# Two token tiles through all 64 experts in place, and first-pass steps inside the front end

## The reference

```python
router_probs = softmax(x @ router_w.T + bias)            # 64 experts
topk_p, topk_i = top_k(router_probs, 6)
topk_p = topk_p / (sum(topk_p) + 1e-09)
# each expert takes its tokens in order, up to C = 768 of them (for 4096 tokens)
expert_out = (silu(expert_in @ w_gate) * (expert_in @ w_up)) @ w_down
sparse = segment_sum(gate * expert_out, token)            # 6 terms per token
h = h + shared_out / 2 + sparse
```

## Time and profile before

| | us |
|---|---|
| median of 3 runs | 575.38 (572.39 to 576.1) |
| span of the profiled execution | 575.5 |
| TensorE busy | 418.5 (73%) |
| VectorE busy | 443.7 (77%) |
| ScalarE busy | 281.9 (49%) |
| GpSimd busy | 405.7 (70%) |

### The profile page before, as it was taken

How to read it: one execution, slowest core, us unless ns; L and a number is a source line. 1 busy time by engine, 2 the same in 40 slices (tenths; PEclk the granted TensorE clock), 3 DMA queues, 4 the chain that set the end, 5 groups by cost and what they waited for, 6 DMA issues and landing times.

```text
span 575.5 us, 11745 instructions
## 1 busy us (share of the span) xinstructions
PE 418.5 (73%) x2715; PEld 351.0 (61%) x2715; DVE 443.7 (77%) x1686; ACT 281.9 (49%) x806; POOL 405.7 (70%) x426
## 2 busy tenths in 40 slices
PE   4487867656673429889999999999999999950000
PEld 3356645545562327789899998889888887630000
DVE  5468999999999664978888668988999887485222
ACT  2026355334443306557777787778767574410000
POOL 7770047777777777777777777777777777777773
PEclk9999878869886556889999999999999798995555
DMA  2899801111114214768888898998899876252221
GB/s 82 202 254 233 165 25 50 52 50 52 51 48 133 82 50 124 210 207 246 250 247 234 237 261 245 242 253 242 246 252 250 237 216 162 53 150 73 60 64 41
DMA packets 128296, 91.13 MB, mean 158 GB/s; under 512 B 15224, under 2 KB 118245, under 8 KB 127974
## 3 DMA queue, kind: packets, MB, share of 16 engines
q1 hardware_dynamic: 64230, 38.63, 26.0%
q0 software_dynamic: 13312, 26.59, 16.0%
q10 hardware_dynamic: 50688, 25.17, 14.6%
HBM read 46.99 MB, written 44.04 MB: 158 GB/s over the span
## 4 chain that ended last, share of the span: by engine, by line
DVE 37%; PE 33%; POOL 15%; issue 9%; DMA 3%; ACT 2%; ACTq 0%; POOLq 0%; DVEq 0%
POOL shared L1107 13%; PE bank L458 11%; PE bank L447 10%; PE bank L438 6%; DVE lanes L1028 3%; DVE gate_junk L925 3%; DVE hid L1022 3%; DVE emb L942 2%; POOL emb L1076 2%; DMA emb<-table_dram,idx 2%; DVE x L778 1%; PE bank L347 1%; DVE struck L817 1%; PE bank L397 1%; DVE shared L717 1%
## 5 line engine op out<-in xcount | busy, mean ns | idle before, releaser
L1092 POOL DMA_INDIRECT x_rows<-x,to_row x192 | 190.3, 991 | 93.4 <-issue 58.0
L1107 POOL DMA_INDIRECT shared<-o_rows,to_got x192 | 182.8, 952 | 58.6 <-issue 57.7
L458 PE MATMUL bank<-w_down,hid 64*128 x768 | 112.5, 287 | 8.9 <-DVE hid L1022 8.6
L626 ACT ACTIVATE w_now<-w_in 128x128 f32 x384 | 87.4, 298 | 55.6 <-issue 26.6
L458 PEld LDWEIGHTS bank<-w_down,hid 64*128 64x128 f32 x768 | 94.1, 190 | 22.1 <-issue 13.2
L447 PE MATMUL bank<-x_t,w_now 128*128 128x128 f32 x768 | 106.8, 284 | 0.1
L447 PEld LDWEIGHTS bank<-x_t,w_now 128*128 128x128 f32 x768 | 98.3, 200 | 0.6 <-ACT x_t L629 0.5
L942 DVE SCALAR_TENSOR_TENSOR emb<-shared,gate_of,emb 128x128 f32<-128x128 f32 x192 | 67.2, 351 | 37.7 <-DMA shared<-o_rows,to_got 32.6
L1022 DVE TENSOR_TENSOR hid<-hid,bank 64x512 f32<-64x512 f32 x96 | 66.2, 690 | 35.4 <-ACT hid L634 32.9
L1028 DVE COPY lanes<-bank 128x512 f32<-128x512 f32 x96 | 66.4, 691 | 3.7 <-PE bank L458 0.7
L634 ACT ACTIVATE hid<-bank 64x512 f32<-64x512 f32 x96 | 56.6, 589 | 25.6 <-PE bank L447 21.4
(11 more groups left out here) (210 smaller groups left out, 595.2 us busy)
## 6 DMA issues: line engine op xcount, KB each, us to landing
lanes<-x_rows SPq DMA_DIRECT2D x384, 64.0 KB
o_rows<-lanes ACTq DMA_DIRECT2D x96, 256.0 KB
x_rows<-hid_s SPq DMA_DIRECT2D x2, 2048.0 KB, 17.7
x_rows<-x,to_row POOLq DMA_INDIRECT x192, 2.2
shared<-o_rows,to_got POOLq DMA_INDIRECT x192
w_in<-gate_t_dram SPq DMA_DIRECT2D x1, 2048.0 KB, 23.5
w_in<-up_t_dram SPq DMA_DIRECT2D x1, 2048.0 KB, 31.1
w_down<-down_t_dram SPq DMA_DIRECT2D x2, 1024.0 KB, 15.6
```

Source lines behind the costliest of these rows:

```text
L458: last = pe.matmul(bank_d[k][:, c * P:c * P + P], hid[k][:, c * P:c * P + P], w[:, bass.ds(at[c], P)], start=(c == 0), stop=(c == GROUP - ...
L626: last = act.activation(w_now[k][:, c, :], w[:, bass.ds(at[c], P)], ACT.Copy)
L1092: pool.indirect_dma_start(x_rows, bass.IndirectOffsetOnAxis(ap=to_row[b][:, t * 8 + j:t * 8 + j + 1], axis=0), x3[b][:, t, :], None, bound ...
L1107: pool.indirect_dma_start(got[n % G_RING][:, j, :], None, o_rows[p], bass.IndirectOffsetOnAxis(ap=to_got[b][:, t * 8 + j:t * 8 + j + 1], a ...
```

## The change

Two things are changed together.

1. **Two dense tiles.** The last two token tiles (tiles 2 and 3 of the last sequence) are neither sent nor fetched. They go through all 64 experts where they lie: 32 dense steps of four experts follow the sparse steps, reading `x3_t` (the transposed tokens, left over from the router of the last sequence) and the weights in place. VectorE adds each expert's output times the token's gate (zero where the expert isn't chosen) to the token's row. The last pass has 768 tokens, so 100 tiles and 25 steps: 93 sparse steps, 125 in all.
2. **The front end.** New tables of ticks, with the first sequence's own row; sequence 1 begins 603 ticks and the others 1500 apart. The first five steps (`STEP_AT`) stand inside the front end: on VectorE step 0 comes after `cols` of sequence 5, step 1 after its `tabs`, step 2 after `rows` of sequence 6, step 3 ahead of the last sequence's `rl`, step 4 behind its `tabs`. The PSUM banks of the steps are dealt anew so that they don't collide with it. Clearing of `x_rows` waits for four gathered sequences, the weight loads for all eight. `fetch` moves to steps 5 to 12, gates to `GATES_IN = (10, 12, 8)`, sums start at step 43.

The diff, cut to its core (the tick tables and the renaming of `PE_AT["x"]` to `at["x"]` are left out):

```diff
@@ -38,35 +38,51 @@
+DENSE = 2
+DENSE_STEPS = DENSE * EXPERTS // GROUP
+TOKENS_OF = [n * SEQ - (DENSE * P if p + 1 == len(PASSES) else 0) for p, n in enumerate(PASSES)]
+TILES_OF = [pass_tiles(n) for n in TOKENS_OF]
...
-FETCH_STEP, STEPS_PER_TOKENS = 43.0, 2.9
+FETCH_STEP, STEPS_PER_TOKENS = 41.0, 2.9
-GATES_IN = (16, 6, 10)
+GATES_IN = (10, 12, 8)
-SPACING = 80
+SPACING, SECOND = 1500, 603
+STEP_AT = (15182, 15750, 16666, 17138, 18718)
@@ -197,7 +215,7 @@
-        bank_x, bank_g, bank_h, bank_d = banks[0:2], banks[2:4], banks[4:6], banks[6:8]
+        bank_x, bank_g, bank_d, bank_h = (bank_e, bank_a0), (bank_a1, bank_b0), (bank_b1, bank_c0), (bank_c1, bank_p)
@@ -222,18 +240,32 @@
+        def front(eng, one, step):
+            for tick in range(LAST_TICK + 1):
+                for b in range(BATCHES):
+                    if tick >= begins(b):
+                        one(eng, b, tick - begins(b))
+                for q, at in enumerate(STEP_AT):
+                    if at == tick:
+                        step(eng, q)
+        def dense_part(q):
+            d, k = divmod(q - STEPS, EXPERTS // GROUP)
+            return d, TILES - DENSE + d, k * GROUP
...
-        FETCH_AT = {1 + b: b for b in range(BATCHES)}
+        FETCH_AT = {len(STEP_AT) + b: b for b in range(BATCHES)}
@@ -261,7 +293,7 @@
-            for b in range(2):
+            for b in range(BATCHES // 2):
                 sp.wait_ge(sem(f"gathered{b}"), 16 * TILES)
@@ -273,6 +305,8 @@
+            for b in range(BATCHES // 2, BATCHES):
+                sp.wait_ge(sem(f"gathered{b}"), 16 * TILES)
...
@@ -432,6 +470,9 @@
         def pe_x_t(pe, q):
             k = q % 2
+            if q < 2:
+                pe.wait_ge(sem(("h", "state")[q]), BATCHES)
@@ -448,9 +494,38 @@
+        def pe_dense_in(pe, q):
+            pe.wait_ge(sem("x3_t"), BATCHES)
+            wait(pe, "hid", q - 1)
+            for c in range(GROUP):
+                last = pe.matmul(bank_g[k][:, c * P:c * P + P], w_in[:, e + c, :], x3_t[:, t * P:t * P + P],
+                                 start=(c == 0), stop=(c == GROUP - 1), skip_group_check=True)
+        def pe_dense_down(pe, q):
+            pe.wait_ge(sem("hid"), q + 1)
+            pe.wait_ge(sem("o_out"), min(q - 1, STEPS))
+            wait(pe, "dense", GROUP * (q - 1 - STEPS))
+            for c in range(GROUP):
+                last = pe.matmul(bank_d[k][:, c * P:c * P + P], hid[k][:, c * P:c * P + P], w_down[:, e + c, :],
+                                 start=(c == 0), stop=(c == GROUP - 1), skip_group_check=True)
@@ -511,28 +591,33 @@
-            front(pe, one)
-            pe.wait_ge(sem("tile_w"), len(PASSES))
-            pe.wait_ge(sem("kept"), 3 * BATCHES)
-            pe.wait_ge(sem("weights"), 16 * 7)
-            for q in range(STEPS + 2):
+            front(pe, one, step)
+            for q in range(len(STEP_AT), ALL_STEPS + 2):
+                step(pe, q)
@@ -907,6 +1000,15 @@ dve_fetch
+            if b + 1 == BATCHES:
+                for d in range(DENSE):
+                    t = TILES - DENSE + d
+                    dve.scalar_tensor_tensor(dense_gate[:, d, :], place[b][:, t, :], 0.0, prob[b][:, t, 2:],
+                                             ALU.is_gt, ALU.mult).then_inc(sem("dense_gate"), 1)
+                    dve.wait_ge(sem("dense_gate"), 2 * d + 1)
+                    dve.tensor_scalar(dense_gate[:, d, :], dense_gate[:, d, :], top_inv[b][:, t:t + 1], None, ALU.mult)\
@@ -1008,20 +1110,28 @@
+            def step(dve, q):
+                if 0 <= q - 1 < ALL_STEPS:
...
+                if q - 2 >= STEPS:
+                    d, t, e = dense_part(q - 2)
+                    dve.wait_ge(sem("pe_down"), q - 1)
+                    dve.wait_ge(sem("dense_gate"), 2 * d + 2)
+                    for c in range(GROUP):
+                        wait(dve, "dense", GROUP * (q - 2 - STEPS) + c)
+                        dve.scalar_tensor_tensor(emb[BATCHES - 1][:, t, :], bank_d[(q - 2) % 2][:, c * P:c * P + P],
+                                                 dense_gate[:, d, e + c:e + c + 1], emb[BATCHES - 1][:, t, :],
+                                                 ALU.mult, ALU.add).then_inc(sem("dense"), 1)
+                if 0 <= q - 2 < STEPS:
...
@@ -1087,7 +1203,7 @@
-                for t in range(TILES):
+                for t in range(TILES - dense_of(b)):
                     for j in range(TOP):
                         pool.indirect_dma_start(
```

More of the change, by code:

```diff
@@ L51 @@
 STEPS = sum(STEPS_OF)
+ALL_STEPS = STEPS + DENSE_STEPS
 X_RING, O_RING, G_RING = 6, 4, 8
 STORE_LAG = 3
-FETCH_STEP, STEPS_PER_TOKENS = 43.0, 2.9
-GATES_IN = (16, 6, 10)
-SPACING = 80
[L62 to L66, removed]
@@ L416, in pe_front @@
                           skip_group_check=True).then_inc(sem("pe_count"), 1)
[L417 removed]
+            if last_of_pass(b) and r == at["tile"]:
                 pe.wait_ge(sem("tile_e"), PASS_OF[b] + 1)
@@ L607, in act_store, with act_step @@
                           quarter(o_out[q % O_RING])).then_inc(sem(f"stored{q % O_RING}"), 16)
+        def act_step(act, q):
+            w = w_in[:, :, :].rearrange("d e f -> d (e f)")
+            if q == 0:
+                act.wait_ge(sem("weights"), 16 * 7)
+            if q < STEPS:
+                k = q % 2
+                if q in STEP0:
+                    act.wait_ge(sem("tile_w"), STEP0.index(q) + 1)
+                at = tile_weights(mybir.EngineType.Activation, q)
+                wait(act, "pe_in", q - 1)
+                for c in range(GROUP):
+                    last = act.activation(w_now[k][:, c, :], w[:, bass.ds(at[c], P)], ACT.Copy)
+                last.then_inc(sem("w_now"), 1)
+                act.wait_ge(sem("pe_x_t"), q + 1)
+                act.activation(x_t[k][:, :], bank_x[k][:, :], ACT.Copy).then_inc(sem("x_t"), 1)
+            if q >= 1:
+                k = (q - 1) % 2
+                act.wait_ge(sem("pe_in"), q)
+                wait(act, "pe_down", q - 2)
+                act.activation(hid[k][:, :], bank_g[k][0:F, :], ACT.Silu).then_inc(sem("silu"), 1)
+            if 0 <= q - STORE_LAG < STEPS:
+                act_store(act, q - STORE_LAG)
         @block.scalar
@@ L986, in one @@
                 dve_front(dve, b, r)
-                if b == 0 and r == DVE_AT["logits"]:
+                if b == 0 and r == DVE_AT[0]["logits"]:
                     dve.wait_ge(sem("pe_prep"), 2)
@@ L1015, in one @@
                     dve.tensor_copy(read_mix[:, :], bank_c0[:, 2 * P:3 * P]).then_inc(sem("prep_done"), 1)
-            front(dve, one)
-            for q in range(STEPS + 2):
-                if 0 <= q - 1 < STEPS:
+            def step(dve, q):
+                if 0 <= q - 1 < ALL_STEPS:
                     k = (q - 1) % 2
@@ L1034, in _ @@
                     dve_sums(dve, *SUM_AT[q])
+            front(dve, one, step)
+            for q in range(len(STEP_AT), ALL_STEPS + 2):
+                step(dve, q)
             late = FIRST_LATE
```

242 lines of the change are left out of this document (138 added, 104 removed).

## The result

The changed kernel takes **583.55 us** (median of 4 runs, 579.57 to 591.53) against 575.15 for the kernel before on the same chip (4 runs, 572.39 to 576.1): ratio 1.0125, 95% interval 1.0067 to 1.0183, slower by 1.25%. The ratio leaves out the run at 591.53, a slow one at a lower granted clock (0.908 against 0.937 to 0.951). The profiled execution has a span of 582.0 us.

What follows compares the result with a forecast made beforehand. GpSimd's sends and fetches bound the kernel before; VectorE's chain was to set the end after: 212.3 + 26.6 + 76.5 + 137.0 + 95.8 + 31.3 = 579.5, say 580 us, against 575.5 before. Range 566 to 594.

Steps and rivals of the forecast that it cites:

- What bounds it: Whole kernel: GpSimd's sends and fetches bound it before; afterwards VectorE's chain does, GpSimd's alone ending at 537 us.
- Step 1: Front end with loop steps 0 to 4: ends at 212.3 us instead of 218.8 (bounds 200 and 218).
- the prediction's own sign ("after 218"): Front end: the predicted mechanism is wrong if it ends before 203 or after 218 us.
- Rival D: ScalarE table switches: 2.66 us each with drain, not 1.28; total 1.4 us more, 581; chance inside the forecast's 0.5.
- Steps 2 and 3: Loop steps 5 to 12, with fetches and gates, 26.6 us; then steps 13 to 43, paced by TensorE, 76.5 us.
- Step 4: Loop steps 43 to 93, with sums of fetched rows: 137.0 us, 5.5 of it waiting (bounds 131.5 and 140).
- Step 5: Dense stage to its last `hid`: 95.8 us (bounds 93 and 102), paced by VectorE at about 3.0 a step.
- Step 6: Shared expert, now uncovered, to the end of the kernel with the result's store: 31.3 us.
- A, GpSimd's gain shows: Front end closes all VectorE idle time, ending at 200 us, the whole at 567: faster; chance 0.22 with smaller gains.
- B, the clock in the dense stage: TensorE's clock falls in the dense stage: 615 us at 1.2 GHz throughout, 592 for a third; chance 0.1.
- C: VectorE's dense stage costs 5% more through handovers, with the front end at 216: 588 us; chance 0.25.
- E: GpSimd's chain still bounds the kernel, at 537 us; chance below 0.02.

Runs made afterwards that it cites:

- the first run on them: The kernel before with clearing of x_rows waiting for four gathered sequences instead of two, weight loads for all eight: 902.51 us, ratio 1.0046.

## Why the prediction was right, point by point

**What bounds it: right.** GpSimd left the chain and VectorE's took over. The last fetch starts at 534.2 (predicted 529), then GpSimd is idle; the experiments with no and one dense tile show both chains and where they cross. The 30.5 us for 12 sends and 12 fetches fewer are of the right kind; the first send came at 66.6, not 71, and these 4.4 us and more were lost again, in two waits for stores, 9.5 us in all, of which the 7.21 between sends and fetches is one. They were in no step of the prediction. They cost nothing here, as the chain has slack.

**Step 1, the front end, was the mis-sized one: 219.7 instead of 212.3.** The order of operations was to bring 4.9 + 2.9 = 7.8 us: with the steps moved away the last cast comes at 210.70 against 218.41, 7.7 earlier. That it fits so well may be luck, as the clock between 127 and 137 was high in that execution. (The third sequence's logits start at 24.01, 3.6 earlier, not 4.9; the rest came elsewhere.)

The front end was to end at 212.3 and ended at 218.2, with the last `hid` of the early steps another 1.5 behind it. Of the 5.9 us, 3.6 are the lower clock before the first early step: the prediction put changes of TensorE's clock in the front end at nothing. The others are the early steps, which cost 3.5 us and not 1.3. What failed there is the sentence that they cost VectorE some 5 us "inside these 12 idle ones" and that a single table load of 1.3 lies on the last sequence's chain. From the seventh sequence's `h2` to the end of the last cast VectorE is busy 32.9 of 44.4 us (173.84 to 218.22), with the steps moved away 29.4 of 40.9 (170.16 to 211.10): 3.5 us of work more, and 11.5 and 11.6 us idle. The idle time stayed, and the work was added in series. By the prediction's own sign ("after 218") its picture of the front end was wrong: 218.2 is just beyond it, and the three other kernels with early steps ended it at 219.5 to 222.3.

ScalarE in the changed kernel, while the last sequence is at its third norm:

```profile
193.03 1.28 ACT L714 ACT_TABLE_LOAD   x1
194.32 0.59 ACT L714 ACTIVATE hid<-bank 64x512 f32<-64x512 f32 x1
...
196.09 0.58 ACT L714 ACTIVATE hid<-bank 64x512 f32<-64x512 f32 x1
...
197.32 1.28 ACT L632 ACT_TABLE_LOAD   x1 [0.65 <-DVE lanes L1138]
198.61 0.20 ACT L632 ACTIVATE ln<-var 128x4 f32<-128x4 f32 x1
198.84 1.28 ACT L634 ACT_TABLE_LOAD   x1
200.13 0.20 ACT L634 ACTIVATE inv<-ln 128x4 f32<-128x4 f32 x1
```

and VectorE beside it:

```profile
195.45 0.69 DVE L1123 TENSOR_TENSOR hid<-hid,bank 64x512 f32<-64x512 f32 x1
196.17 0.69 DVE L1138 COPY lanes<-bank 128x512 f32<-128x512 f32 x1
200.37 0.16 DVE L744 TENSOR_TENSOR t<-inv 128x4 f32<-128x4 f32 x1 [3.50 <-ACT inv L634]
```

The way back from Silu takes two loads, one for Ln and one for Exp. Both lie ahead of `inv`, and before them ScalarE first serves two steps: VectorE waits 3.50 us where without early steps it waits 0.51, and has a `hid` and a copy more in front, 1.3. From the last sequence's `h2` to its `x3` it is 8.4 us (192.55 to 200.96) instead of 4.0 (188.98 to 193.02): 4.4 us are lost in this one place, and 0.8 are regained behind it. The first early step has three loads on ScalarE (176.89, 178.79, 180.31), but these delay nothing that lasts: the two kernels are 3.7 us apart at the seventh sequence's `h2`, before them, and 3.6 at the eighth's. From 160 to 218.6 there are 11 loads, before 4: seven more, where the prediction had about four. With the set preloaded (the trace of the run on one of the two other chips) the second load is gone:

```profile
309.44 0.59 ACT L714 ACTIVATE hid<-bank 64x512 f32<-64x512 f32 x1
310.05 1.28 ACT L716 ACT_TABLE_LOAD   x1
311.34 0.20 ACT L632 ACTIVATE ln<-var 128x4 f32<-128x4 f32 x1
311.58 0.20 ACT L634 ACTIVATE inv<-ln 128x4 f32<-128x4 f32 x1
```

What that is worth in time is open.

Rival D asked for the price of one switch. From the load's start to the activation's it is 1.29 us (197.32 to 198.61), and the next load starts 0.03 us behind that activation (198.61 + 0.20, 198.84). The Trainium skill (ScalarE: Activation LUTs, What ACT_TABLE_LOAD costs) adds a drain of some 1.4 us to it; the trace shows no such time ahead of a load or behind it, so the measurement decides. The switch was dearer than assumed by being two loads, not by a drain.

**Steps 2 and 3: right** within 0.5 us. They had rows of before of the same kind.

**Step 4: 133.4 instead of 137.0.** The parts gave 131.5, and 5.5 us of waiting for `silu` were added after the 7.1 of before. Measured are 1.8 us of waiting there. So the waits did not grow with the fuller VectorE, they nearly went. The clock has a part in it: in this stage it was 1.00 in the changed kernel, and 0.97 on average before, with 2.8 of the 7.1 us of waits from 444 us on, where it was 0.86 to 0.96. The rest is not shown; TensorE (131.2 of 136.1 us busy) and VectorE (128.3) are both near full there.

**Step 5: the mechanism right, 93.6 instead of 95.8.** Four chained sums were to take 1.53 us start to start. Ahead of `hid` they do (504.24 to 505.79, 1.55), ahead of a half sum they take 1.42 (500.95 to 502.37). Of the 22 half sums 20 stand in a step with four sums (the two others are in the first two steps, which still have the copy): 20 x 0.11 = 2.2 us, the whole difference. That the stage runs by VectorE and not by TensorE is shown by the copy in place of the sums.

**Step 6: right**, 31.95 against 31.3. No DMA is waited for at the end.

**The rivals.** A, GpSimd's gain shows: with `hid` 4 at 219.7 it fell here; but it would have needed only one dense tile fewer: then the kernel is 21.1 us faster than before. B, the clock in the dense stage: it stayed at 1.00 with TensorE busy 69.6 of 91.1 us, so the comparison with the front end (65.3 of 96.3 at 0.86) misled. C named 588 from a front end at 216 and 5% on the dense stage: its first half happened, and more, its second had the other sign. The chances do not fit together: 0.5 for the forecast and 0.22, 0.1, 0.25 and 0.02 for rivals A, B, C and E make 1.09. The three for slower, same and faster make 1.

So the sum, 579.5, came within 2.5 us of the span of 582.0 by a miss of +7.4 us in step 1 and of -4.9 us in the others together (+0.45, -0.2, -3.6, -2.2, +0.65): that is luck, and each step's own error says more than that of the sum. The median lies another 1.5 us above the span; before the two were 0.4 apart (575.15 and 575.5), and the prediction took no difference.

## What to carry to other kernels

Where one chain ends 60 us before the other, these 60 us are a budget: compute what each unit of shifted work takes from one and adds to the other (here 14.4 us off GpSimd for the first tile, 6 sends and 6 fetches, against 27.4 us onto VectorE's chain for the second) and stop where they meet, at one tile and not two. Work placed into idle time of a serial stretch need not be hidden by it: here 3.5 us of work made the stretch 3.5 us longer, since it stands in the same queues as the serial chain, and still it paid, as it saved 12.0 behind. For ScalarE one counts the table loads of the way there and of the way back, by function. And before a difference between two traces is put down to an edit, one looks where it begins: half of the 7.1 us here began before the first moved instruction.

## What the hardware showed

- After a Silu, Ln and then Exp each load a table, 1.28 us apiece (197.32 and 198.84), although with a preload one load serves both. The Trainium skill (ScalarE: Activation LUTs, Table sets: the hidden batching unit) counts one load for ln followed by exp; without the preload the traces show two.
- Dependent 128x128 sums on VectorE run at 0.38 us start to start, from PSUM as from SBUF, and four take 1.42 to 1.55 us, where one copy of 128x512 takes 0.60 to 0.73 to the next start.
- The granted clock stayed at 1.00 through 91 us in which TensorE was busy 76% (69.6 of 91.1 us), with idle pieces of about 1 us in 20 of the 32 steps.
- The same instructions in the same order got a granted clock of 0.53 in one kernel's execution and 1.00 in another's from 127 to 137 us; a pair of products (L404) takes 0.63 us there against 0.39. The distance between the two grew from 1.5 to 3.7 us there.
- Two chips ran the same programs 1.6 times as long. In the trace of the first run on them, busy times other than TensorE's are equal within 1%, and 31.3% of the chain of waits lies in pieces of up to 31 us that nothing in the profile releases.
